# Recutting the first stage of a two-network graph kernel: x loaded in both layouts, the mean taken off by a matmul, squares summed by TensorE

## The reference, cut to what matters

```python
h = jnp.maximum(_layernorm(x), 0.0)                     # x: 4096 x 128
x = x + _L0_gnn_ref(h, adj, embed, layer, embed_bias, layer_bias)
h = jnp.maximum(_layernorm(x), 0.0)
x = x + _L1_gnn_ref(h, adj, beta1, beta2)               # two masked attention layers

# _L0_gnn_ref:
h1 = h_mul(h, embed); h1 = h_add(h1, embed_bias)        # h_mul = exp_map_zero(log_map_zero(h) @ W)
neigh = exp_map_zero(adj @ log_map_zero(h1))            # adj: 4096 x 4096
out = h_add(h_mul(concatenate((h, neigh), 1), layer), layer_bias)
```

## Time and profile before

| | |
|---|---|
| time, median of 3 runs | 976.91 us (976.67 to 977.71) |
| time of the profiled execution | 978.14 us |
| its span in the profile | 976.6 us |
| first `aggregate` matmul (L469) starts | 57.41 us |
| PE busy | 929.2 us (95%) |
| DVE busy | 818.8 us (84%) |
| ACT busy | 511.2 us (52%) |
| DMA queue of x and adj, share of 16 engines | 57.6% |

### The profile page before, as it was taken

One profiled execution on the slowest core, in us unless ns is written; L12 is line 12 of the kernel. 1 busy time (PEld: TensorE's weight loads), 2 busy tenths in 40 slices (PEclk: granted clock), 3 DMA queues, 4 the chain that ended last, 5 costly groups with the idle time before them and its releaser, 6 DMA issues.

```text
span 976.6 us, 22955 instructions
## 1 busy us (share of the span) xinstructions
PE 929.2 (95%) x9012; PEld 695.3 (71%) x9012; DVE 818.8 (84%) x2110; ACT 511.2 (52%) x756; POOL 8.0 (1%) x21
## 2 busy tenths in 40 slices
PE   2989999999996999999999999999999999999996
PEld 2944444444444878888888888778888888888885
DVE  7891888888889987888989898998778887888887
ACT  1711122212126685766656667787565565656564
POOL 0000000000000000000000000000000000000000
PEclk9899999999998999999999999999999999999999
DMA  8338988888861445565465555545565655665630
GB/s 301 143 118 285 307 285 287 277 295 283 301 229 44 174 173 207 196 246 212 179 235 192 222 217 193 180 167 217 197 217 198 246 197 204 221 232 189 246 142 36
DMA packets 29971, 207.26 MB, mean 212 GB/s; under 512 B 3632, under 2 KB 4272, under 8 KB 5296
## 3 DMA queue, kind: packets, MB, share of 16 engines
q1 hardware_dynamic: 28224, 203.44, 57.6%
q0 software_dynamic: 640, 2.10, 0.5%
q10 hardware_dynamic: 1008, 0.33, 0.1%
HBM read 203.75 MB, written 2.10 MB: 211 GB/s over the span
## 4 chain that ended last, share of the span: by engine, by line
PE 69%; DVE 22%; issue 5%; ACT 3%; DMA 1%; DVEq 0%; POOL 0%; SPq 0%; POOLq 0%
PE s_ps L622 17%; PE s_ps L608 10%; PE acc_ps L469 6%; PE acc_ps L675 6%; PE acc_ps L671 6%; PE acc_ps L673 6%; PE acc_ps L652 5%; PE acc_ps L648 5%; PE acc_ps L650 5%; DVE small L1132 1%; DVE small L1134 1%; DVE small L1133 1%; DVE work L1647 1%; ACT work L990 1%; PE s_ps L427 1%
## 5 line engine op out<-in xcount | busy, mean ns | idle before, releaser
L990 ACT ACTIVATE work<-s_ps,beta_bias,beta_scale 128x1024 f32<-128x1024 f32 x144 | 173.4, 1204 | 217.0 <-PE s_ps L622 216.9
L469 PE MATMUL acc_ps<-ring,set 128*128 128x512 f32 x512 | 223.8, 596 | 3.2 <-DVE set L1245 3.2
L1665 DVE SCALAR_TENSOR_TENSOR h_all<-ring,s_ps 128x1024 f32<-128x1024 f32 x112 | 136.7, 1221 | 65.5 <-PE s_ps L608 64.3
L469 PEld LDWEIGHTS acc_ps<-ring,set 128*128 128x128 f32 x512 | 96.8, 191 | 120.3 <-issue 117.6
L1647 DVE TENSOR_TENSOR work<-work 128x1024 f16<-128x1024 f32 x96 | 132.5, 1380 | 5.4 <-ACT work L1000 5.4
L1000 ACT ACTIVATE work<-work 128x1024 f16<-128x1024 f32 x96 | 131.5, 1369 | 3.2 <-DVE work L1655 0.2
L1655 DVE SCALAR_TENSOR_TENSOR work<-ring,work 128x1024 f32<-128x1024 f32 x96 | 116.8, 1217 | 0.0
L622 PE MATMUL s_ps<-xt 128*128 128x512 f16 x432 | 106.4, 382 | 3.8 <-ACT work L990 3.0
L622 PE MATMUL s_ps<-set 128*128 128x512 f16 x432 | 105.0, 379 | 0.5 <-ACT work L990 0.5
L671 PE MATMUL acc_ps<-set,work 128*128 128x129 f16 x576 | 102.4, 219 | 2.7 <-DVE accs L1682 2.7
L671 PE MATMUL acc_ps<-src,work 128*128 128x129 f16 x576 | 103.5, 220 | 1.4 <-DVE work L1655 1.4
(11 more groups left out here) (260 smaller groups left out, 1723.2 us busy)
## 6 DMA issues: line engine op xcount, KB each, us to landing
ring<-in_adj_t SPq DMA_DIRECT2D x192, 1024.0 KB, 5.0
x_sb<-in_x SPq DMA_DIRECT2D x4, 512.0 KB, 7.2
out<-x_sb POOLq DMA_DIRECT2D x8, 256.0 KB, 2.8
w<-in_layer ACTq DMA_DIRECT2D x2, 64.0 KB, 8.1
w<-in_embed ACTq DMA_DIRECT2D x1, 64.0 KB, 4.2
eb<-in_embed_bias ACTq DMA_DIRECT2D x1, 64.0 KB, 6.9
lb<-in_layer_bias ACTq DMA_DIRECT2D x1, 64.0 KB, 7.9
beta<-in_beta ACTq DMA_DIRECT2D x2, 0.5 KB, 7.2
```

Of the source, the lines that this page charges most:

```text
L469: last = nc.tensor.matmul(agg, v_sb[:, jb, :], ring[:, k, b, :], start=jb == 0, stop=jb == NB - 1)
L990: nc.scalar.activation(values[x.n % VR], score_ps, ACT.Exp, bias=beta_bias[:, x.la:x.la + 1], scale=beta_scale[:, x.la:x.la + 1]).then_inc ...
L1665: V.scalar_tensor_tensor(turned[x.off % MR].rearrange("p (b j) -> p b j", b=CB), ring[:, x.mir_tile % AR, :, ds(x.h * HB * P, HB * P)], 0. ...
```

## The change

`x_t`, the transpose of x, becomes a further input. SP loads it in four DMAs of 512 KB, interleaved with the four of x, all ahead of the `adj` tiles. The order is x_t 0, x_t 1, x 0, x_t 2, x 1, x_t 3, x 2, x 3.

The transposes and the normalised rows are gone. PE multiplies x_t by the constant `centre` (identity minus 1/128) in one 128x512 matmul for each group, which takes the mean off; ACT takes the ReLU into `ht_sb`, and squares that into `sq_sb`; PE sums the squares by 128x1 matmuls against ones into `hh_ps`. The factor 1/deviation (`ext`) is applied later: DVE multiplies `hh_ps` by its square, and the arctanh factor and the output of `h1_out` by it. The bias product is the 129th column of the product with `embed`, so the 128x1 products with `web` are gone. `g_out` copies 129 columns.

On PE the order is columns two groups ahead, lengths, and one `products` for each two groups; products 4 to 7 follow after all lengths. On ACT it is ReLU one group ahead, squares, and a `g_out` after each two groups, the rest after. `h1_out` has four scaled copies for one plain copy of a group; three of them now stand ahead of the tanh, four between tanh and the next logarithms. PE runs four idle matmuls (EARLY_WARM) at the start, and WARM is 30 rather than 10, behind a wait for `closing`, which DVE raises in the middle of the row arithmetic (L1227).

```diff
-    WARM = 10
+    WARM = 30
+    EARLY_WARM = 4
...
-        ht_ps = [acc_ps[:, 2 + i, :] for i in range(2)]
+        ht_ps = [acc_ps[:, 1 + i, :] for i in range(3)]
... SP: x_columns(0); for each i: x_columns(i + 1), x_rows(i)
+            for _ in range(EARLY_WARM):
+                nc.tensor.matmul(acc_ps[:, 3, 0:P], ident[:, :], ident[:, :], start=True, stop=True)
+            pe.wait_ge(centre_made, 1)
+            def h_columns(r):
+                if r % 2 == 0:
+                    pe.wait_ge(xt_in[r // 2], 16)
+                wait(pe, ht_copied, r - 2)
+                nc.tensor.matmul(ht_ps[r % 3], centre, xt_in_sb[:, ts(r, CH)], start=True, stop=True)\
+                    .then_inc(ht_done, 1)
+            def h_lengths(r):
+                pe.wait_ge(ht_squared, r + 1)
+                for b in blocks(r):
+                    last = nc.tensor.matmul(hh_ps[:, b:b + 1], sq_sb[:, ts(b, P)], ones[:, 0:1], start=True, stop=True)
+                last.then_inc(hh_done, 1)
+            def products(r):
+                wait(pe, g_copied, r - 1)
+                for b in range(CB):
+                    last = nc.tensor.matmul(g_ps[r % 2][:, b // 2, ts(b % 2, PW)], ht_sb[:, ts(r * CB + b, P)],
+                                            w1[:, 0:PW], start=True, stop=True)
+                last.then_inc(g_done, 1)
+            h_columns(0)
+            h_columns(1)
             for r in range(NC):
+                if r + 2 < NC:
+                    h_columns(r + 2)
+                h_lengths(r)
+                if r == 1:
+                    pe.wait_ge(web_made, 1)
+                if r % 2:
+                    products(r // 2)
+            for r in range(NC // 2, NC):
+                products(r)
...
+            pe.wait_ge(closing, 1)
             for _ in range(WARM):
... ACT
+            h_out(0)
             for r in range(NC):
+                if r + 1 < NC:
+                    h_out(r + 1)
+                h_squares(r)
+                if r % 2:
+                    g_out(r // 2)
+            for r in range(NC // 2, NC - 1):
+                g_out(r)
             log_terms(sm(4, NB), sm(5, NB), sm(6, NB))
             g_out(NC - 1)
+            for r in range(0, 3):
+                h1_out(r)
             on(ACT.Tanh, sm(5, NB), sm(4, NB))
-            for r in range(NC // 2):
+            for r in range(3, NC - 1):
                 h1_out(r)
             log_terms(sm(4, NB), sm(5, NB), sm(6, NB))
-            for r in range(NC // 2, NC):
-                h1_out(r)
+            h1_out(NC - 1)
... DVE
-            for r in range(NC):
-                for b in blocks(r):
-                    ins = V.tensor_scalar(scr_b[:, b, :], x_sb[:, b, :], mean_var[:, b, 0:1], small[:, 1, b:b + 1],
-                                          ALU.subtract, ALU.mult)
-                ins.then_inc(xs_ready, 1)
-            for b in range(NB):
-                ins = V.scalar_tensor_tensor(v_sb[:, b, :], scr_b[:, b, :], 0.0, scr_b[:, b, :],
-                                             ALU.max, ALU.mult, accum_out=hh[:, b:b + 1])
+            inv_sqrt(ext[:, :], sm(0, NB), sm(2, NB))
+            step(V.tensor_tensor(sm(3, NB), ext[:, :], ext[:, :], ALU.mult))
+            dve.wait_ge(hh_done, NC)
+            ins = V.tensor_tensor(hh[:, :], hh_ps, sm(3, NB), ALU.mult)
```

More of the change, by code:

```diff
@@ L24, with build @@
 from contextlib import ExitStack
-def build(nc, x, adj, adj_t, embed, layer, embed_bias, layer_bias, beta1, beta2, out):
+def build(nc, x, x_t, adj, adj_t, embed, layer, embed_bias, layer_bias, beta1, beta2, out):
     f32, f16, b16, i32 = mybir.dt.float32, mybir.dt.float16, mybir.dt.bfloat16, mybir.dt.int32
@@ L101, in build @@
         adj_rows = work[:, 0:N]
-        scr_a = work[:, 0:NB * F].rearrange("p (b f) -> p b f", f=F)
+        scr_a = work[:, 0:NB * PW].rearrange("p (b w) -> p b w", w=PW)
+        gb_sb = scr_a[:, :, F]
+        sq_sb = set1[:, 0:N]
+        xt_in_sb = xt0[:, :, :].rearrange("p s n -> p (s n)").bitcast(f32)
         scr_b = xt0[:, :, :].rearrange("p s n -> p (s n)").bitcast(f32)[:, 0:NB * F].rearrange("p (b f) -> p b f", f=F)
@@ L113, in build @@
         at_sb = accs[:, :, :].rearrange("p b w -> p (b w)")[:, 0:CH]
+        centre = at_sb[:, 0:P]
         unused = accs[:, :, :].rearrange("p b w -> p (b w)")[:, CH:2 * CH].rearrange("p (b f) -> p b f", f=F)
-        w1 = sb("w1", [F, 2 * F])
+        w1 = sb("w1", [F, 2 * F + 1])
+        web = w1[:, F:F + 1]
         w2 = sb("w2", [F, F])
@@ L139, in build @@
         ht_sb = src0_all[:, 0:2 * N].bitcast(f32)
-        web = sb("web", [F, 1])
         ones_h = sb("ones_h", [P, P], f16)
@@ L154, in build @@
         acc_ps = ctx.enter_context(nc.psum_tensor("acc_ps", [P, CB, 512], f32))
-        g_ps = [s_ps[:, i, 0:CH].rearrange("p (b f) -> p b f", f=F) for i in range(2)]
+        g_ps = [s_ps[:, i, :].rearrange("p (k n) -> p k n", k=2)[:, :, 0:2 * PW] for i in range(2)]
         h1_ps = [s_ps[:, i // 2, ts(i % 2, CH)].rearrange("p (b f) -> p b f", f=F) for i in range(4)]
-        gb_ps = acc_ps[:, 0, 0:NB]
+        hh_ps = acc_ps[:, 0, 0:NB]
         w_ps = s_ps[:, 0, 0:CH].rearrange("p (b f) -> p b f", f=F)
         xt_ps = s_ps[:, 1, 0:CH]
-        ht_ps = [acc_ps[:, 2 + i, :] for i in range(2)]
+        ht_ps = [acc_ps[:, 1 + i, :] for i in range(3)]
         rows_ps = s_ps[:, 0, CH:2 * CH].rearrange("p (b f) -> p b f", f=F)
@@ L179, in build @@
         x_in = [sem(f"x_in{i}") for i in range(XP)]
+        xt_in = [sem(f"xt_in{i}") for i in range(XP)]
         embed_in = sem("embed_in")
@@ L189, in build @@
         mean_made = sem("mean_made")
-        xs_ready = sem("xs_ready")
+        centre_made = sem("centre_made")
+        deviations_made = sem("deviations_made")
+        closing = sem("closing")
         web_made = sem("web_made")
@@ L194, in build @@
         g_done = sem("g_done")
-        gb_done = sem("gb_done")
+        ht_squared = sem("ht_squared")
+        hh_done = sem("hh_done")
         h1_done = sem("h1_done")
@@ L321, in _, with x_columns, x_rows @@
         def _(sp):
+            def x_columns(i):
+                sp.dma_start(xt_in_sb[:, ts(i, N // XP)], x_t[:, ts(i, N // XP)]).then_inc(xt_in[i], 16)
+            def x_rows(i):
+                sp.dma_start(x_sb[:, ts(i, NB // XP), :], x_v[:, ts(i, NB // XP), :]).then_inc(x_in[i], 16)
+            x_columns(0)
             for i in range(XP):
-                sp.dma_start(x_sb[:, ts(i, NB // XP), :], x_v[:, ts(i, NB // XP), :]).then_inc(x_in[i], 16)
+                if i + 1 < XP:
+                    x_columns(i + 1)
+                x_rows(i)
             sp.wait_ge(x_in[XP - 1], 16)
@@ L409, in _ @@
             pe.wait_ge(consts_made, 6)
[L410 to L420, removed]
-            for r in range(NC):
-                if r + 1 < NC:
-                    h_transposes(r + 1)
-                pe.wait_ge(ht_copied, r + 1)
+            for _ in range(EARLY_WARM):
+                nc.tensor.matmul(acc_ps[:, 3, 0:P], ident[:, :], ident[:, :], start=True, stop=True)
@@ L431, in _ @@
+            h_columns(1)
+            for r in range(NC):
+                if r + 2 < NC:
+                    h_columns(r + 2)
+                h_lengths(r)
+                if r == 1:
                     pe.wait_ge(web_made, 1)
-                for b in blocks(r):
-                    last = nc.tensor.matmul(gb_ps[:, b:b + 1], ht_sb[:, ts(b, P)], web[:, :], start=True, stop=True)
-                last.then_inc(gb_done, 1)
+                if r % 2:
+                    products(r // 2)
+            for r in range(NC // 2, NC):
+                products(r)
@@ L440, in _ @@
                 for b in range(CB):
-                    last = nc.tensor.matmul(h1_ps[r % 4][:, b, :], ht_sb[:, ts(r * CB + b, P)], w1[:, F:2 * F],
+                    last = nc.tensor.matmul(h1_ps[r % 4][:, b, :], ht_sb[:, ts(r * CB + b, P)], w1[:, ds(PW, F)],
                                             start=True, stop=True)
@@ L742, in _ @@
                 .then_inc(embed_in, 16)
-            for dst, s in ((w1[:, F:2 * F], layer[0:F, :]), (w2[:, :], layer[F:2 * F, :]),
+            for dst, s in ((w1[:, ds(PW, F)], layer[0:F, :]), (w2[:, :], layer[F:2 * F, :]),
                            (lb[:, :], layer_bias.rearrange("(a f) -> a f", a=1).to_broadcast([P, F])),
@@ L767, in g_out @@
                     q = r * CB + b
-                    nc.scalar.activation(h1_sb[:, q, :], g_ps[r % 2][:, b, :], ACT.Square,
+                    nc.scalar.activation(h1_sb[:, q, :], g_ps[r % 2][:, b // 2, ds(b % 2 * PW, F)], ACT.Square,
                                          accum_out=small[:, 10, q:q + 1])
-                nc.scalar.activation(scr_a[:, ts(r, CB), :], g_ps[r % 2], ACT.Copy).then_inc(g_copied, 1)
+                nc.scalar.activation(scr_a[:, ts(r, CB), :].rearrange("p (k b) w -> p k (b w)", k=2), g_ps[r % 2],
+                                     ACT.Copy).then_inc(g_copied, 1)
             def h1_out(r):
```

(41 more changed lines are left out.)

15 lines of the change are left out of this document (7 added, 8 removed).

## The result

The changed kernel is slower: 987.31 us (983.52 to 988.94, 6 runs) against 977.84 (976.67 to 980.9, 6 runs) for the kernel before, ratio 1.0087, 95% interval 1.006 to 1.0114. The direction is the forecast's; the size is not. 9.5 us later is nearly three times the 3.4 forecast and lies above the range. Run once more, in a job with three of its variants, it took 988.28 (988.15 to 988.7), ratio 1.0116 (1.0102 to 1.0131).

The account below looks back on a forecast made before the run. PE bounds the aggregation, so its start at the first L469 matmul decides. Last copy 3.7 later, tanh 1.4 later, warm-up 1.7 gained: 3.4 us later, 976.9 + 3.4 = 980.3 us; range 973.2 to 985.5.

Parts of the forecast that it names:

- the clock in the rounds: PE's three rounds of two groups: first at full clock, other two at half, 23.0 us; bounds 17.5 and 26.2.
- Rival 4: Before the aggregation: half clock from the start to the last lengths, +9.8 us, 986.7; chance 0.12.
- Loads, statistics, adj tiles: Input loads and DVE statistics: `ext` stands at about 24, 6 us later, adj tiles end at 46; all free.
- Rival 5: Loads: x_t quarters at twice the spacing (3 us), `ext` at 33, DVE the bound; near +1 us, chance 0.04.
- First product: PE's start through products 0: ends at 13.4 us if the clock has risen by 10.1, at 16.6 if not.
- A round is a sum: ACT and PE work per two groups adds up, not a maximum: 6.1 us full clock, 9.3 half; last 5.3 or 7.6.
- Products 3 to the last copy: ACT's five g_out and logarithms after the rounds: 7.9 us, taken as 8.8 with PE at half clock.
- The tanh: Last copy to tanh read, three h1_out ahead: 5.8 us, 1.4 later; at half clock 8.1, 3.8 later.
- Warm-up: Idle matmuls from `closing` to L469: PE idles 1.7 in place of 3.24, the clock holds, 1.7 us gained.
- Rival 1: The clock holds in all three rounds and the kernel is faster: -3.0 us, 973.9; chance 0.22.

Follow-up runs that it names:

- second profile: The changed kernel, unedited, run again in a later job beside three of its variants: 988.28 us, ratio 1.0116; profiled span 986.8.
- first profile: The changed kernel against the kernel before, first measurement (987.31 us, ratio 1.0087); the profiled execution is its fastest, 983.52 us, span 981.9.

## Why the prediction missed

Its path and its sum were right. The step that failed is the clock in the rounds: I took one round at full clock and two at half, and in the profile that stands for most runs all three were at half. That case had a number, 3.4 + 3.2 = +6.6 (983.5), inside the range; the other 3.6 us to the +10.2 of that profile are slow rounds and a tanh that took longer than I had them. Rival 4, slow from the start, has nearly the measured number (+9.8, 986.7), but its mechanism did not come about: it needs the first product at 16.6, and it came at 14.1. That nearness is a coincidence.

- **Loads, statistics, adj tiles: free.** Right. DVE stands ready and waits 11.49 us for the lengths (L1263). Rival 5 is out.
- **First product.** 13.4 forecast; the first g_out begins at about 14.1 in both profiles. 0.7 short, and near the fast start rather than the 16.6 of the slow one.
- **A round is a sum.** Right, and shown by moving g_out. At full clock 6.5, 6.5, 5.7 measured for 6.1, 6.1, 5.3: the squares read from SBUF are 0.67 with their tail, and hand-overs are more. At half clock 9.65, 9.93, 8.23 for 9.3, 9.3, 7.6.
- **The clock in the rounds: the step that failed.** "I take the first round fast and the other two slow: 6.1 + 9.3 + 7.6 = 23.0." In the second profile the clock was at half from 17.2 to 44.5 us, three slow rounds, 27.8. That is 4.8 of the 6.8 us missing there (10.2 later for 3.4): 3.2 because the first round was slow too, 1.6 because a slow round is longer than summed. In the first profile the clock came back from 23.1 to 26.5, and the rounds make 23.1. That the sum was met there is luck: 7.25, 7.63 and 8.23 are not one round at full clock and two at half. The rows of before spoke for a clock that stays low: at 41.0 it fell and was at half until 47.8 although PE ran 128x128 products from 41.61 on the earlier trace rows. They don't settle it, for in the first profile it came back after 3.4 us, in the middle of a round.
- **Products 3 to the last copy.** 8.8 forecast. From the start of g_out 3 (41.95) to the end of the last copy (50.13) it took 8.2 in the second profile: 0.6 less.
- **The tanh: mis-sized.** 1.4 later forecast, 2.9 and 3.1 measured (in the second profile it is read 7.5 us behind the last copy). "PE has just run products, so I take 1.4" was wrong. PE idles 2.2 us ahead of h1, the clock is at half from 47.0 to 50.4 in the first profile, and the first three h1_out start 1.5 and 1.7 apart, near the 1.8 of the half-clock bound, 3.8 (timeline of the first profile):

```profile
46.87 1.14 ACT L812 ACTIVATE set<-s_ps,ext 128x128 f32<-128x128 f32 x4 [1.31 <-PE s_ps L472]
48.34 1.14 ACT L812 ACTIVATE set<-s_ps,ext 128x128 f32<-128x128 f32 x4 [0.34 <-PE s_ps L472]
...
50.05 1.14 ACT L812 ACTIVATE set<-s_ps,ext 128x128 f32<-128x128 f32 x4 [0.57 <-PE s_ps L472]
```

- **Warm-up.** Right: 1.7 off the first chunk in every profile that has it. In time 3 when added to the old kernel (2 between the lowest runs), 2 when taken from the changed one.
- **Adding up, second profile:** 0.7 + 4.8 - 0.6 on the last copy (50.1 for 45.2), 1.7 on the tanh, 0.2 from rounding: 6.8. With the forecast's 3.4 that is the 10.2 by which the spans differ.
- **Rival 1, a clock that holds,** did not come about by itself. Filled with wide work it did, and gave 1.0014 rather than the -3.0 us I gave it: each round was 0.4 longer, the clock still fell at h1 (half from 41.3 to 44.7) and once more at 318 us. The Trainium skill (TensorE: Matmul & The Clock Gate, Why this matters for your kernels) names idle gaps as what drops the clock. The trace of the run with 128x1 filling does not agree: from 18 to 45 us PE is busy 27.0 of 27 us, and the mean granted clock is 0.56.

What stays open: why the clock returns within the rounds in some runs and not in others, and how much of the 3 us between the warm-up's medians is the warm-up and how much the share of the old kernel's runs in its upper group.

## What to carry to other kernels

When work moves from one engine to another, write down each engine's order for one period and follow the hand-overs round: if A's next piece stands behind B's last and B's behind A's, the period is the sum of both, and placing one item later may be worth more than the whole change. Count wide matmuls apart from 128x1 products when judging TensorE's clock, and give a stretch whose clock is in doubt its half-clock length in the middle of the range, not in the tail; here that was the case in most runs. Put the instruction that the critical chain asks for, with its table load, ahead of copies that nobody waits for.

## What the runs showed of the hardware

A TensorE that is busy all the time can be at half clock: 17.00 of 17 us busy at a granted clock of 0.51 in the run with 128x1 filling, where the wide matmuls of the rounds stand between 128x1 products. The same program differs by 5 us from run to run, and of the 4.9 between its two profiles 4.7 lie in three rounds whose clock differs. This holds for the kernel before too: in the first job its runs lie from 976.65 to 982.48, in two groups some 4 us apart. The profiled execution of its warm-up variant shows one way to such a distance: by the durations of its matmuls, the full clock first comes at 35 us, for 27 in the kernel before (the clock column shows 1.00 there, as the prediction notes), and its first aggregation matmul starts at 61.13 for 57.41, although the work up to h1 is the same. The clock can also fall with no wait of TensorE ahead of it: in the run with 128x1 filling it fell at 28.3 us, with PE busy 3.97 of the 4 us from 24 to 28.
